# One kernel of feed-forward, token mixing and feed-forward: four pieces of work moved in the mixing stage

## The chip, the cores and the metric

The kernel runs on one core of a Trainium2 chip. Its time is the device time of one launch in microseconds (us); the time before is 3143.79 us, the median of three runs (3139.49 to 3144.29).

A core has five engines that run side by side, each with its own list of instructions in a fixed order: TensorE (PE in the profile, with its weight loads as PEld), VectorE (DVE), ScalarE (ACT), GpSimd (POOL) and SyncE (SP, which here only issues DMAs). They meet at semaphores: an instruction that waits holds up all that stand behind it on its engine.

## The reference

Three layers act on 8192 tokens of 256 channels (8 sequences of 1024):

```
x = x + 0.5 * ffn(layernorm(x))      # 16 experts, top 2 of them per token, capacity 1280 rows each
x = x + attn(layernorm(x))           # token mixing, RWKV-6
x = x + 0.5 * ffn(layernorm(x))      # the same experts once more
```

The middle layer is the one that the change touches:

```
xx  = previous token - x                       # "differences"
xxx = x + xx * maa_x
lora = tanh(xxx @ maa_w1)                      # 5 strips of 32
xf  = x + xx * (maa_f + lora_f @ maa_w2_f)     # f = w, k, v, r, g: the five mixes
r, k, v = xr @ Wr, xk @ Wk, xv @ Wv
g = tanh(xg @ gate_w1) @ gate_w2               # the gates
w = exp(-exp(time_decay + tanh(xw @ decay_w1) @ decay_w2))
y_t = r_t (S + u k_t v_t);  S = w_t S + k_t v_t     # one state of 64 x 64 per head, 4 heads
out = (groupnorm(y) * ln_g + ln_b) * g @ Wo
```

The router of the third layer (layernorm, logits over 16 experts, top 2, place in the expert) is computed in the same stage, on the rows that the mixing has finished.

## The kernel before

The program is a row of stages: constants, routing a, experts a, mixing together with routing b (`mix_and_route`), experts b. Only the mixing stage is changed. In the profiled execution it lies from about 1205 to 2215 us.

The stage works in 16 groups of 512 tokens (`NG`, `GT`), four tiles of 128 rows each. It is a software pipeline written out by hand: for step s in -2 to 18, each engine runs a fixed list of pieces for five groups at once. X = s+2 is the group that comes in (layernorm, transposition, differences, first mixes), F = s+1 gets its other mixes, keys, values, queries and decays, L = s goes through the eight levels of the products inside a tile, K = s-1 gets states, outputs, gates and Wo, R = s-2 is routed, and Z = s-3 has its rows scattered to the experts' slots. The order of the `if live(..)` blocks in each engine's loop is the order of execution; no scheduler stands behind it.

What ties the engines within a step:

- The levels. `level(L, n)` on TensorE (L1757) needs `take(n-1)` on VectorE (copy_predicated, L1203 for n=0, L1208 for the others) and the two multiplications `decay_right` and `decay_left` (L1221, L1232; together `factors`). `factors(L, n)` in its turn needs `level(L, n+1)`. So TensorE and VectorE hand the work to and fro eight times in a step, and the rest of both engines' work is put between.
- The PSUM banks. Four banks, a to d, serve all products; the list `order` says which product uses which bank after which. Each `fill` waits until the product before it in its bank is drained. Here it matters that "L" (the router's logits) follows "Y0" in bank b, where Y0 is drained by ScalarE's square (L1607), and that "V0" and "V1" (the values) follow "M8" and "M9" (the two halves of the last mix, for r), which are drained by VectorE's `mix_in` (L1179).
- The last mix. `mixes_of_rest` (L1857) writes M8 and M9 in two passes with a wait on `rest_half` between them.
- Buffers. `xx` exists once: `differences(X)` (L1167 and two of L1171) overwrites what `mix_in(F, 8)` and `mix_in(F, 9)` still read, and so stands behind them.
- GpSimd's list in the middle of a step: four indirect DMAs of the routed rows (L1515), the additions of mixes 8 and 9 (`mix_add`, L1464), the gate product `gate(K)` (L1504: Y times G), the root of the variances (L1487), four more indirect DMAs, and the additions of mixes 0 to 3.
- ScalarE's list: it copies the finished outputs Y (L1606) and their squares (L1607), then the logits, values and queries. In the first half of the step it copies keys (L1630), normalises the group that comes in (L1575) and copies transposed rows out of PSUM (L1563), the routed ones (`untie(ROUTE, ..)`, to `m_ygT`) after `keys` and `normalise`.

## Time and profile before

| | us |
|---|---|
| time, median of 3 | 3143.79 |
| the profiled execution's own time | 3144.1 |
| its span in the trace | 3142.4 |
| TensorE busy | 2773.4 (88%) |
| VectorE busy | 2017.5 (64%) |
| ScalarE busy | 1572.8 (50%) |
| GpSimd busy | 1256.9 (40%) |

The shares are those of the whole span. The two expert stages take some 1900 us of it, nearly all with TensorE busy. A change of the mixing stage has to be read from the steps of that stage. In the trace's lines the program's names stand with their stage's prefix, so `m_xx` is `xx` of the mixing stage; a line in brackets behind an instruction gives the idle time of its engine just before it and what ended it. The granted clock (PEclk) is TensorE's, as a share of its full speed.

### The profile page before, as it was taken

Reading aid. Unit: us, or ns where it says so; the run is one execution under the profiler, and the core shown is the slowest. Engines: PE = TensorE matmul, PEld = TensorE weight load, DVE = VectorE, ACT = ScalarE, POOL = GpSimd, SP = SyncE. Lnnn points to the kernel's source line nnn. Section 1 sums busy time; section 2 is a strip of 40 time slices with the busy share of each in tenths; the row PEclk is TensorE's granted clock in tenths of the full one; section 3 lists DMA queues with packets and bytes.
Section 4 is the critical chain, followed back from the end, with each engine's and each line's share of the span. In section 5 each row is a group of like instructions: output and inputs, shape, how many; then the busy total and the mean of one; then the engine's idle time right before and its main releaser. Section 6 shows DMA issues by size and latency. Waiting matters only on the chain. (4 is left out here: it accounts for less than half of the span.)

```text
span 3142.4 us, 63449 instructions
## 1 busy us (share of the span) xinstructions
PE 2773.4 (88%) x21936; PEld 2236.8 (71%) x21936; DVE 2017.5 (64%) x4620; ACT 1572.8 (50%) x2733; POOL 1256.9 (40%) x1072
## 2 busy tenths in 40 slices
PE   6354999999999995899899999974899999999997
PEld 6343888888888882566566666653788888888886
DVE  5354665666666653688888888863566666666664
ACT  5232665656665652344444444421556656656653
POOL 2652332222322223456676666644122322223233
PEclk9999999999999997999999999966899999999998
DMA  9924454544545527101111111001644545545444
GB/s 344 310 74 107 87 95 80 89 87 86 88 80 88 94 28 260 50 21 39 41 43 36 49 36 43 31 30 46 125 87 86 92 78 89 90 85 87 79 75 146
DMA packets 540964, 281.26 MB, mean 90 GB/s; under 512 B 397591, under 2 KB 503131, under 8 KB 540480
## 3 DMA queue, kind: packets, MB, share of 16 engines
q1 hardware_dynamic: 478624, 202.67, 25.8%
q0 software_dynamic: 57888, 75.16, 14.0%
q8 instruction: 127, 2.08, 0.3%
q10 hardware_dynamic: 4224, 0.52, 0.1%
q14 instruction: 101, 0.83, 0.1%
HBM read 150.83 MB, written 146.41 MB: 95 GB/s over the span
## 5 line engine op out<-in xcount | busy, mean ns | idle before, releaser
L763 POOL DMA_INDIRECT acc_a<-ae_ob,ae_to x160 | 260.2, 1626 | 675.7 <-ACT ae_ob L712 623.2
L763 POOL DMA_INDIRECT acc_b<-be_ob,be_to x150 | 243.5, 1623 | 636.3 <-ACT be_ob L712 534.0
L730 ACT ACTIVATE be_h<-be_pH,b 128x512 f32<-128x512 f32 (+1 forms) x384 | 236.8, 617 | 359.8 <-PE be_pH L657 334.4
L730 ACT ACTIVATE ae_h<-ae_pH,b 128x512 f32<-128x512 f32 (+1 forms) x384 | 236.8, 617 | 344.8 <-PE ae_pH L657 327.6
L1464 POOL TENSOR_TENSOR m_xf<-m_tmp,m_xT 128x512 f32<-128x512 f32 x160 | 181.3, 1160 | 150.6 <-DVE m_tmp L1179 150.5
L1757 PEld LDWEIGHTS m_PP<-m_RP,m_KS 64*64 64x64 f32 x6656 | 124.2, 142 | 106.9 <-issue 105.8
L1757 PE MATMUL m_PP<-m_RP,m_KS 64*64 64x64 f32 x6656 | 139.4, 229 | 56.3 <-DVE m_A L1208 49.4
L1515 POOL DMA_INDIRECT slots_b<-m_row,m_sidx x128 | 137.7, 1076 | 117.7 <-issue 117.7
L464 POOL DMA_INDIRECT slots_a<-ar_row,ar_sidx x128 | 125.8, 982 | 130.8 <-issue 105.9
L1179 DVE SCALAR_TENSOR_TENSOR m_tmp<-m_B,m_ch,m_xx 128x512 f32<-128x512 f32 x160 | 111.9, 741 | 71.3 <-PE m_B L1847 37.9
L657 PE MATMUL ae_pH<-ae_xT0h,ae_w_0h 128*128 128x512 f32 (+1 forms) x256 | 88.1, 344 | 53.8 <-DVE ae_xT0l L839 51.4
L684 PE MATMUL be_pO<-be_w,be_hT3h 128*128 128x512 f32 x320 | 118.5, 400 | 4.2 <-DVE be_hT3l L856 4.1
L1221 DVE TENSOR_TENSOR m_RP<-m_RP,m_tot 128x512 f32<-128x512 f32 x96 | 95.4, 994 | 39.3 <-PE m_PP L1757 31.4
L684 PE MATMUL be_pO<-be_w,be_hT0h 128*128 128x512 f32 x320 | 119.0, 402 | 1.3 <-DVE be_hT0l L856 1.2
L684 PE MATMUL ae_pO<-ae_w,ae_hT0h 128*128 128x512 f32 x320 | 118.5, 401 | 1.4 <-DVE ae_hT0l L856 1.3
L684 PE MATMUL be_pO<-be_w,be_hT1h 128*128 128x512 f32 x320 | 117.3, 397 | 1.8 <-DVE be_hT1l L856 1.7
L684 PE MATMUL ae_pO<-ae_w,ae_hT3h 128*128 128x512 f32 x320 | 117.1, 396 | 0.1
L684 PE MATMUL ae_pO<-ae_w,ae_hT1h 128*128 128x512 f32 x320 | 117.1, 396 | 0.0
L684 PE MATMUL be_pO<-be_w,be_hT2h 128*128 128x512 f32 x320 | 117.0, 396 | 0.0
L684 PE MATMUL ae_pO<-ae_w,ae_hT2h 128*128 128x512 f32 x320 | 117.0, 396 | 0.0
L657 PE MATMUL be_pH<-be_xT0h,be_w_0h 128*128 128x512 f32 (+1 forms) x256 | 88.2, 344 | 32.6 <-DVE be_xT0l L839 30.8
L856 DVE TENSOR_TENSOR ae_hT0l<-ae_h,ae_hT0h 128x512 fp32r<-128x512 f32 (+1 forms) x96 | 57.9, 603 | 90.0 <-ACT ae_hT0h L730 90.0
(343 smaller groups left out, 9009.5 us busy)
## 6 DMA issues: line engine op xcount, KB each, us to landing
ae_stage<-in_w SPq DMA_DIRECT2D x64, 512.0 KB, 3.5
be_stage<-in_w SPq DMA_DIRECT2D x64, 512.0 KB, 3.6
slots_a<-empty SPq DMA_DIRECT2D x5, 4160.0 KB, 25.0
slots_b<-empty SPq DMA_DIRECT2D x5, 4160.0 KB, 31.5
ae_xq<-slots_a SPq DMA_DIRECT2D x252, 64.0 KB
be_xq<-slots_b SPq DMA_DIRECT2D x252, 64.0 KB
ar_xin<-in_x SPq DMA_DIRECT2D x16, 512.0 KB, 10.1
m_xin<-acc_a SPq DMA_DIRECT2D x16, 512.0 KB, 4.8
```

Source lines behind the costliest of these rows:

```text
L464: pool.indirect_dma_start(S.slots[tag][:, :], bass.IndirectOffsetOnAxis(ap=sidx[u][:, q, k:k + 1], axis=0), row[u][:, q, :], None, bounds_ ...
L657: t = pe.matmul(pH[c % 2][:, 0:SIZES[b]], w1[u][a][:, k, f * P:(f + 1) * P], xT[(u * BLOCKS + b) % 2][z][:, k, 0:SIZES[b]], start=(n == 0) ...
L684: pe.matmul(to[:, q % 2, :], hT[s][HI][:, ts], w2[u][:, f, :, :].rearrange("p s d -> p (s d)"), start=(f == 0), stop=(f == FC - 1), skip_g ...
L730: t = act.activation(dst[:, 0:SIZES[b]], pH[c % 2][:, 0:SIZES[b]], ACT.Gelu, bias=S.b1[:, bass.ds(i * (2 * FC) + (u * FC + f), 1)])
L763: pool.indirect_dma_start(S.acc[tag][:, :], bass.IndirectOffsetOnAxis(ap=to[m][:, q:q + 1], axis=0), ob[m][:, q, :], None, bounds_check=T ...
L856: dve.tensor_tensor(hT[s][LO][:, 0:SIZES[b]], h32[c % 2][:, 0:SIZES[b]], hT[s][HI][:, 0:SIZES[b]], ALU.subtract).then_inc(h_split, 1)
L1179: drains(dve.scalar_tensor_tensor(out=tmp[m % TMP][:, :], in0=bank(f"M{m}", g)[:, :], scalar=ch[:, 1 + f, k:k + 1], in1=xx[:, k, :], op0=A ...
L1221: dve.tensor_tensor(rp[:, :, 1, :], rp[:, :, 1, :], pieces(l)[:, :, 0:1].to_broadcast([P, DC * GT >> (l + 1), 1 << l]), ALU.mult).then_inc ...
L1464: pool.tensor_tensor(xf[f][:, k, :], tmp[m % TMP][:, :], xT[g % 2][:, k, 1:GT + 1], ALU.add).then_inc(mixed, 1)
L1515: pool.indirect_dma_start(S.slots["b"][:, :], bass.IndirectOffsetOnAxis(ap=sidx[w][:, q, k:k + 1], axis=0), row[w][:, q, :], None, bounds_ ...
L1757: t = pe.matmul(PP[c * N:c * N + N, h, to], ks[rows, r, ts], rp[rows, r, ss], start=True, stop=True, skip_group_check=True)
```

## The change

Four pieces move; no instruction is added or taken away.

1. VectorE: `differences(X)` goes ahead of `mix_in(F, 8..9)`. For this `xx` is doubled, and `xxx` gets no buffer of its own any more but uses `wl`, the buffer of the clamped decays. Two waits come with it: `differences` waits for `w_ready` (the decays of the group before are read out of `wl`), `clamp` for "LG" (the products that read `xxx` are done). The wait for M9 of the group before goes.
2. GpSimd: `gate(K)` goes ahead of the additions of mixes 8 and 9. Two of the four DMAs in front of it go to the block behind the root.
3. TensorE: the logits stand between the two passes of `mixes_of_rest`.
4. TensorE and ScalarE: the routed rows are turned, and copied out, ahead of the keys; beside it the first decay product (`rate(F, 0)`) goes ahead of `level(L, 2)`.

```diff
-        xx = sb("xx", [P, DC, GT])
-        xxx = sb("xxx", [P, DC, GT])
+        xx = [sb(f"xx{u}", [P, DC, GT]) for u in range(2)]
...
+        xxx = wl[:, :].rearrange("p (c t) -> p c t", c=DC)
...
                 def differences(g):
                     untied(dve, IN, g)
-                    drained(dve, "M9", g - 1)
...
                     filled(dve, "LG", g - 1)
+                    hold(dve, w_ready, g)
...
                 def clamp(g, k):
                     hold(dve, w_ready, g)
+                    filled(dve, "LG", g)
...
                     keep(L, 4)
+                    if live(X):
+                        differences(X)
                     if live(F):
                         for m in range(8, 10):
                             mix_in(F, m)
-                    if live(X):
-                        differences(X)
...
                     if live(Z):
-                        scatter(Z, (0, 1))
+                        scatter(Z, (0,))
+                    if live(K):
+                        gate(K)
                     if live(F):
                         for m in range(8, 10):
                             mix_add(F, m)
                     if live(K):
-                        gate(K)
                         root_spread(K)
                     if live(Z):
-                        scatter(Z, (2, 3))
+                        scatter(Z, (1, 2, 3))
...
+                    if live(R):
+                        filled(act, "O1", K - 1)
+                        untie(ROUTE, R, xTr[:, :, :])
                     if live(F):
                         keys(F)
                     if live(X):
                         normalise(X)
-                    if live(R):
-                        filled(act, "O1", K - 1)
-                        untie(ROUTE, R, xTr[:, :, :])
...
-                    if live(L):
-                        level(L, 2)
                     if live(F):
                         rate(F, 0)
+                    if live(L):
+                        level(L, 2)
                     if live(L):
                         gates(L, 0)
+                    if live(R):
+                        turn_route(R)
                     if live(F):
                         project(F, "K", Wk, 1)
-                    if live(R):
-                        turn_route(R)
...
                     if live(F):
-                        mixes_of_rest(F)
+                        mixes_of_rest(F, 0)
                     if live(R):
                         logits(R)
+                    if live(F):
+                        mixes_of_rest(F, 1)
```

VectorE in the middle of a step, before, from the factors of level 3 to those of level 4:

```order
L1221 TENSOR_TENSOR m_RP<-m_RP,m_tot 128x64x8
L1232 TENSOR_TENSOR m_KS<-m_KS,m_tot 128x64x8
L1208 COPY_PREDICATED m_A<-m_lev,m_PP 128x64x8
L1179 SCALAR_TENSOR_TENSOR m_tmp<-m_B,m_ch,m_xx 128x512 x2
L1167 TENSOR_TENSOR m_xx<-m_xT 128x1024
L1171 SCALAR_TENSOR_TENSOR m_xxx<-m_xx,m_ch,m_xT 128x512 x2
L1255 TENSOR_REDUCE m_var<-m_Y 128x16
L1258 TENSOR_SCALAR m_mvar<-m_var 128x16
L1221 TENSOR_TENSOR m_RP<-m_RP,m_tot 128x32x16
```

The same stretch of VectorE in the changed kernel, where two lines of code more stand ahead of these (so L1223 is what L1221 was) and `m_wl` holds `xxx`:

```order
L1223 TENSOR_TENSOR m_RP<-m_RP,m_tot 128x64x8
L1234 TENSOR_TENSOR m_KS<-m_KS,m_tot 128x64x8
L1210 COPY_PREDICATED m_A<-m_lev,m_PP 128x64x8
L1167 TENSOR_TENSOR m_xx<-m_xT 128x1024
L1172 SCALAR_TENSOR_TENSOR m_wl<-m_xx,m_ch,m_xT 128x512 x2
L1180 SCALAR_TENSOR_TENSOR m_tmp<-m_B,m_ch,m_xx 128x512 x2
L1257 TENSOR_REDUCE m_var<-m_Y 128x16
L1260 TENSOR_SCALAR m_mvar<-m_var 128x16
L1223 TENSOR_TENSOR m_RP<-m_RP,m_tot 128x32x16
```

The subtraction and the two instructions for `xxx` have passed the two of the last mix. GpSimd in the same part of the step, before:

```order
L1497 TENSOR_TENSOR m_G<-m_G,m_ln_g 128x1024
L1515 DMA slots_b<-m_row,m_sidx 20480x260 x4
L1464 TENSOR_TENSOR m_xf<-m_tmp,m_xT 128x512 x2
L1504 TENSOR_TENSOR m_Y<-m_Y,m_G 128x1024
L1487 TENSOR_TENSOR m_rvar<-m_mvar,m_minus_half 128x16
L1515 DMA slots_b<-m_row,m_sidx 20480x260 x4
```

GpSimd in the changed kernel:

```order
L1499 TENSOR_TENSOR m_G<-m_G,m_ln_g 128x1024
L1517 DMA slots_b<-m_row,m_sidx 20480x260 x2
L1506 TENSOR_TENSOR m_Y<-m_Y,m_G 128x1024
L1466 TENSOR_TENSOR m_xf<-m_tmp,m_xT 128x512 x2
L1489 TENSOR_TENSOR m_rvar<-m_mvar,m_minus_half 128x16
L1517 DMA slots_b<-m_row,m_sidx 20480x260 x6
```

The gate product has passed the additions, and two DMAs have gone behind the root. TensorE between levels 4 and 5, before:

```order
L1757 MATMUL m_PP<-m_RP,m_KS 64x64 x32
L1819 MATMUL m_B<-m_St,m_RP 128x64 x16
L1857 MATMUL m_B<-m_lorag,m_maa_w2r 128x256 x4
L1926 MATMUL m_B<-m_ygT,m_rw 32x128 x8
L1897 MATMUL m_B<-m_Wv,m_xf 128x256 x8
```

TensorE in the changed kernel:

```order
L1760 MATMUL m_PP<-m_RP,m_KS 64x64 x32
L1822 MATMUL m_B<-m_St,m_RP 128x64 x16
L1861 MATMUL m_B<-m_lorag,m_maa_w2r 128x256 x2
L1929 MATMUL m_B<-m_ygT,m_rw 32x128 x8
L1861 MATMUL m_B<-m_lorag,m_maa_w2r 128x256 x2
L1900 MATMUL m_B<-m_Wv,m_xf 128x256 x8
```

The four products of the last mix are parted two and two, with the logits (`m_rw`) between them. In the trace each of these products shows as two records, so a count there is twice the one here.

## Rows read from the trace of the kernel before

**Rows 1.** Timeline of VectorE: start us, us, engine, line; first copy of steps 1 and 14
```profile
1307.53 1.31 DVE L1203 COPY_PREDICATED m_A<-m_diag,m_PP 128x1024 f32<-128x1024 int32 x1 [0.45 <-PE m_PP L1757]
...
2016.39 1.31 DVE L1203 COPY_PREDICATED m_A<-m_diag,m_PP 128x1024 f32<-128x1024 int32 x1 [0.47 <-PE m_PP L1757]
```
**Rows 2.** Timeline of TensorE in step 5 (1522 to 1577 us), middle part
```profile
1543.40 1.16 PE L1757 MATMUL m_PP<-m_RP,m_KS 64*64 64x64 f32 x64
...
1546.42 0.70 PE L1857 MATMUL m_B<-m_lorag,m_maa_w2r 32*128 32x256 f32 x4
1547.99 0.70 PE L1857 MATMUL m_B<-m_lorag,m_maa_w2r 32*128 32x256 f32 x4 [0.87 <-PE m_B L1857]
1548.62 0.64 PE L1926 MATMUL m_B<-m_ygT,m_rw 128*32 128x128 f32 x16
1549.62 3.69 PE L1897 MATMUL m_B<-m_Wv,m_xf 128*128 128x256 f32 x16 [0.35 <-DVE m_tmp L1179]
1553.24 1.16 PE L1757 MATMUL m_PP<-m_RP,m_KS 64*64 64x64 f32 x64
...
1560.53 1.79 PE L1757 MATMUL m_PP<-m_RP,m_KS 64*64 64x64 f32 x64 [2.43 <-DVE m_A L1208]
...
1567.94 1.09 PE L1765 MATMUL m_PT<-ident,m_Y 128*128 128x128 f32 x8
```
**Rows 3.** Timeline of VectorE in the same step
```profile
1544.68 0.69 DVE L1221 TENSOR_TENSOR m_RP<-m_RP,m_tot 128x512 f32<-128x512 f32 x1 [0.40 <-PE m_PP L1757]
...
1545.89 0.68 DVE L1208 COPY_PREDICATED m_A<-m_lev,m_PP 128x512 f32<-128x512 int32 x1
1548.72 1.41 DVE L1179 SCALAR_TENSOR_TENSOR m_tmp<-m_B,m_ch,m_xx 128x512 f32<-128x512 f32 x2 [2.14 <-PE m_B L1857]
1550.23 5.50 DVE L1167 TENSOR_TENSOR m_xx<-m_xT 128x1024 f32<-128x1024 f32 x1
1555.77 1.42 DVE L1171 SCALAR_TENSOR_TENSOR m_xxx<-m_xx,m_ch,m_xT 128x512 f32<-128x512 f32 x2
...
1558.46 0.69 DVE L1221 TENSOR_TENSOR m_RP<-m_RP,m_tot 128x512 f32<-128x512 f32 x1
```
**Rows 4.** Timeline of GpSimd in the same step
```profile
1546.64 0.97 POOL L1515 DMA_INDIRECT slots_b<-m_row,m_sidx  x1 [0.30 <-issue]
...
1550.17 2.17 POOL L1464 TENSOR_TENSOR m_xf<-m_tmp,m_xT 128x512 f32<-128x512 f32 x2
1552.27 2.38 POOL L1504 TENSOR_TENSOR m_Y<-m_Y,m_G 128x1024 f32<-128x1024 f32 x1
```
**Rows 5.** The subtraction over all steps: ns min/median/max, first and last start us
```profile
L1167 DVE TENSOR_TENSOR m_xx<-m_xT x16: 1225/4956/5503, 1217.4 to 1990.4; 128x1024 f32<-128x1024 f32 x16
```
**Rows 6.** Timeline of ScalarE in the same step: outputs Y and their squares
```profile
1547.77 0.60 ACT L1607 ACTIVATE m_Y<-m_B 128x512 f32<-128x512 f32 x1
1548.26 0.59 ACT L1606 COPY m_Y<-m_B 128x512 f32<-128x512 f32 x1
```
**Rows 7.** Timeline of TensorE in the next step, first half
```profile
1584.09 1.16 PE L1757 MATMUL m_PP<-m_RP,m_KS 64*64 64x64 f32 x64 [0.82 <-DVE m_A L1208]
...
1593.58 1.07 PE L1765 MATMUL m_PT<-ident,m_KR 128*128 128x128 f32 x8 [0.60 <-ACT m_ygT L1563]
```
**Rows 8.** Timeline of TensorE in a late step
```profile
1880.61 5.92 PE L1897 MATMUL m_B<-m_Wv,m_xf 128*128 128x256 f32 x16
...
1891.24 0.97 PE L1757 MATMUL m_PP<-m_RP,m_KS 64*64 64x64 f32 x50
```
**Rows 9.** Stretches: busy us (count) by engine, then PEclk, DMA share, GB/s
```profile
1562.00:1565.00 3.00, 3.00 (x16) 1.41 (x11) 2.76 (x10) 0.19 (x1) 2.25 (x3) 0.63 0.14 50
1878.00:1885.00 7.00, 6.56 (x30) 4.63 (x31) 5.20 (x3) 2.57 (x6) 6.37 (x6) 0.52 0.16 57
```
**Rows 10.** Timelines of VectorE and GpSimd in an early step without row scatters
```profile
1388.97 4.23 DVE L1171 SCALAR_TENSOR_TENSOR m_xxx<-m_xx,m_ch,m_xT 128x512 f32<-128x512 f32 x2
...
1389.85 2.80 POOL L1504 TENSOR_TENSOR m_Y<-m_Y,m_G 128x1024 f32<-128x1024 f32 x1
```

More of the change, by code:

```diff
@@ L1849, in mixes_of, with mixes_of_rest @@
                                            tile_position=(32 * j, 0)), f"M{m}", g)
[L1851 removed]
+                def mixes_of_rest(g, a):
                     drained(pe, "LG", g)
[L1853 to L1863 removed]
+                    if a:
+                        pe.wait_ge(rest_half, g * 2 + 2)
+                    for k in range(DC):
+                        j = k ^ a
+                        b = bank(f"M{8 + k}", g) if a else fill(f"M{8 + k}", g)
+                        t = pe.matmul(b[:, j * GT // 2:(j + 1) * GT // 2], maa_w2r[32 * j:32 * j + 32, k * P:(k + 1) * P],
+                                      lorag[32 * j:32 * j + 32, :], start=True, stop=True, tile_position=(32 * j, 0))
+                        if a:
+                            fills_up(t, f"M{8 + k}", g)
+                        else:
+                            t.then_inc(rest_half, 1)
                 def narrow(g):
```

18 lines of the change are left out of this document (4 added, 14 removed).

## The prediction

> **What bounds the kernel now.** I first took the page's engine shares: TensorE is the fullest engine, but in the mixing stage the work goes to and fro between TensorE and VectorE, so shares say little, and I went on to the timelines of a step. The first copy of a step starts at 1307.53 in step 1 and at 2016.39 in step 14 [rows 1]: 13 steps in 708.9 us, 54.5 us each. All of this is on the path, since the experts of the last layer start when the stage has ended. Only steps 1 to 13 have both a group that comes in and a gate product, so only there do the first two moves bear together.
>
> In step 5 the reader is to follow one chain. Level 4 starts on TensorE at 1543.40, the two passes of the last mix at 1546.42 and 1547.99 with 0.87 idle between them, the logits at 1548.62, the values at 1549.62 after a wait for VectorE, level 5 at 1553.24. Level 6 then waits 2.43 us for VectorE [rows 2]. VectorE was late because its subtraction took 5.50 us [rows 3], while the same instruction takes 1.225 us at its shortest [rows 5]. It started at 1550.23, when GpSimd had just begun two additions and the gate product behind them (1550.17 to 1554.65) [rows 4]; it ended at 1555.73, about 1.1 us after the last of these. So the subtraction stood still while GpSimd worked, and then ran at its usual speed.
>
> Behind the 2.43 us wait level 6 takes 1.79 us, other levels 1.16 [rows 2], and from 1562 to 1565 the granted clock averages 0.63: TensorE, which had stood idle, had fallen from 2.4 to 1.2 GHz for part of the time [rows 9]. In late steps it goes otherwise: the clock falls in the sparse stretch of the last mix and the logits (0.52 on average from 1878 to 1885 [rows 9]), the values take 5.92 instead of 3.69 us, and level 6 follows without a wait [rows 8]. The step is as long either way.
>
> **The change part by part.** No instruction is added, so what counts are waits.
>
> *Differences ahead, gate ahead.* VectorE's copy of level 3 ends at 1546.57 and it then idles 2.14 us [rows 3]; the subtraction and `xxx` fit there: 1.22 + 1.42 = 2.64 us, if nothing blocks them. GpSimd does only DMAs then [rows 4]. The new waits for `w_ready` and "LG" are for work finished earlier. The last mix may then start on VectorE at 1549.2 at the soonest. Behind it only `spread` is left before level 5's factors, which leaves the 5.50 + 1.42 us of [rows 3] out of that place. Six DMAs instead of four stand behind the root; GpSimd has idle time behind them, cost 0.
>
> *Logits between the passes.* This looks like a filler for the 0.87 us. But the logits use the bank of Y0 and must wait for ScalarE's square, which ends at 1547.77 + 0.60 = 1548.37 [rows 6]; the second pass started at 1547.99 before [rows 2] and now comes only behind the logits. So this edit delays it: logits at 1548.37, 0.63 long (1547.99 to 1548.62 is the pass, 1548.62 to 1549.25 the logits by the same measure), second pass at 1549.0, 1.0 us later than before. Between the start of the second pass and `mix_in` lie 1548.72 - 1547.99 = 0.73 us, and from there to the values 0.90 us: the values at 1550.63, 1.0 us later than 1549.62. The bounds: the 0.87 us gained if Y0 is drained before the first pass ends, 1.0 lost as computed; I take the loss of 1.0, since its rows stand in this step.
>
> *Rows ahead of the keys, decay product ahead of level 2.* In the next step level 2 waits 0.82 us for VectorE, and the transposition of the incoming rows 0.60 us for ScalarE's copy of the routed ones [rows 7]. The decay product fills idle time, the copy leaves the place between normalisation and transposition. The keys come 1.0 us later and so does ScalarE's normalisation in part. Bounds 0 and 0.6; no such wait stands in step 5, so I take 0.3.
>
> *The sum for a step.* Level 4 and all behind it move by -0.3, the values by +1.0 beside: they start at 1550.3, and level 5 at 1553.24 + 0.7 = 1553.94. Factors 4 follow a level's start by 1544.68 - 1543.40 = 1.28: 1555.22 instead of 1558.46 [rows 2, 3]. From these factors to the transposition of Y VectorE works without a gap worth naming, 1567.94 - 1558.46 = 9.48: now 1564.70. That is 3.2 us earlier. TensorE has level 6 at 1553.94 + (7.29 - 2.43) = 1558.80 and keeps up if its clock is high.
>
> *The clock.* The sparse stretch from level 4's end to the values gets longer and has two waits: for the square, and 0.9 for the first `mix_in`. The rows of late steps show a fall just there. Its cost is 0 at least; at most 2.23 (values, 5.92 against 3.69) and some 1.0 for the second pass and logits at half rate, 3.2 in all. The nearest rows are the values' own, so I take 2.2. Net: 3.2 - 2.2 = 1.0 us a step, 13 steps, 13 us. The profiled execution took 3144.1 us (span 3142.4 and 1.7 around it), 0.3 above the median, which I leave out: 3131.
>
> **The rivals.**
>
> *The clock stays up.* For it: step 5 had a high clock through this same stretch with idle time of 1.2 us. Against: the stretch is now emptier. Then 3.2 x 13 = 42 us: 3102.
>
> *The step keeps its length.* The clock takes back all of it. For it: waits before level 6 and slow values are exchanged for each other in the trace and the step stays at 54.5. Cost 3.2 of 3.2: 3144.
>
> *`xxx` is blocked by the gate product.* This ends slower. In an early step the two instructions of `xxx` took 4.23 us while the gate product started at 1389.85 beside them, 2.80 long [rows 10]: one of them waited for it. In the changed kernel the gate product no longer stands behind additions and starts when the second copy of Y is done, 1548.85 - 0.3 = 1548.55 [rows 6]. The second `xxx` instruction starts at 1546.2 (a copy's 0.6 behind, 0.3 earlier) + 1.26 + 0.71 = 1548.2. It wins by some 0.35 us. If the gate product's request comes before the first `xxx` instruction ends at 1548.2, the second waits for 2.38 us, ends at 1551.3, the values start 0.9 later at 1552.2 instead of 1550.3: 1.9 us later. With the clock's full 3.2 that is 3.2 - 1.9 - 3.2 = -1.9 a step, or 25 us: 3169; with 2.2 for the clock it is -0.9, or 12 us: 3156. I put it at 3160, between them. It decides if Y is ready 0.35 us sooner or the differences start that much later. The Trainium skill, page "SBUF — State Buffer", section "SBUF: two separate sides", says that a VectorE instruction with two SBUF inputs and a GpSimd instruction that reads SBUF contend for one pair of ports as an exclusive lock, held for the whole instruction by whichever started first. By that rule the move only changes who meets whom, and every step in which the gate product comes first pays; the trace agrees with the blocking (5.50 against 1.225).
>
> **How the numbers follow.** Apart from 0.2% (6.3 us; less than that is no change for this measurement) the boundary lies at 3137.5 and 3150.1. The forecast has 0.43, of it 0.37 faster and 0.06 within the bound; the high clock 0.17, all faster; the unchanged step 0.20, 0.18 of it the same and 0.02 slower; the blocked `xxx` 0.20, 0.19 slower and 0.01 the same. Sum: faster 0.54, same 0.25, slower 0.21. The likeliest case alone reaches from 3118 to 3140. The range leaves out half of the high clock's case and half of the blocked one: 3104 to 3158.
>
> **What the profile after would show.** Right: the subtraction at 1.2 to 1.5 us right behind level 3's copy; no wait of 2.4 us before level 6; the logits after 1 to 1.5 us of idle TensorE behind the first pass, their releaser ScalarE's square; the values at 5 to 6 us in most steps; first copies 53 to 54 us apart. Wrong: `xxx` at over 3 us for its two instructions (blocked), values at 3.7 in all steps and copies 51.3 apart (high clock), copies still 54.5 apart, or a new wait that none of this names, such as level 4's take behind the keys or level 5 behind a blocked `spread`.

## The result, and the profile after

The changed kernel takes 3254.59 us (median of four runs, 3250.09 to 3257.55), the kernel before 3143.00 beside it: a ratio of 1.0356, 95% interval 1.0338 to 1.0374. It is slower by 112 us, where 13 us faster was predicted and 3158 was the end of the range. The profiled execution has a span of 3251.0 us, 108.6 more than before. By the first copies of the steps, 5.4 us of this are lost ahead of step 0 (two traces of the kernel before differ there by 6.8) and 103.4 between step 0 and step 15 (907.9 us instead of 804.5). The last stage is as long as it was.

First copies of the steps (VectorE's timeline: start, duration, then what ended the idle time before). They answer to [rows 1]:

```profile
1319.19 1.32 DVE L1205 COPY_PREDICATED m_A<-m_diag,m_PP 128x1024 f32<-128x1024 int32 x1 [0.45 <-PE m_PP L1760]
...
1554.44 1.31 DVE L1205 COPY_PREDICATED m_A<-m_diag,m_PP 128x1024 f32<-128x1024 int32 x1 [0.47 <-PE m_PP L1760]
1616.95 1.31 DVE L1205 COPY_PREDICATED m_A<-m_diag,m_PP 128x1024 f32<-128x1024 int32 x1 [0.47 <-PE m_PP L1760]
...
2117.50 1.32 DVE L1205 COPY_PREDICATED m_A<-m_diag,m_PP 128x1024 f32<-128x1024 int32 x1 [0.47 <-PE m_PP L1760]
```

Steps 1 to 13 take 61.4 us each instead of 54.5, step 5 takes 62.5. The first of them do not: 55.6 in step 1 and 54.7 in step 2 (52.3 and 52.6 before), and 62.5 from step 3 on. Step 3 is the first with a group Z whose rows are scattered. So two losses can be told apart at sight: 2 to 3 us a step that is there without DMAs, and a jump of 7.8 us from step 2 to step 3, when the DMAs come, where the kernel before jumps by 2.1.

Step 5 on TensorE, as in [rows 2]:

```profile
1576.27 1.16 PE L1760 MATMUL m_PP<-m_RP,m_KS 64*64 64x64 f32 x64
...
1579.29 0.70 PE L1861 MATMUL m_B<-m_lorag,m_maa_w2r 32*128 32x256 f32 x4
1580.70 0.64 PE L1929 MATMUL m_B<-m_ygT,m_rw 128*32 128x128 f32 x16 [0.71 <-ACT m_Y L1610]
1581.27 0.70 PE L1861 MATMUL m_B<-m_lorag,m_maa_w2r 32*128 32x256 f32 x4
1585.17 5.86 PE L1900 MATMUL m_B<-m_Wv,m_xf 128*128 128x256 f32 x16 [3.20 <-DVE m_tmp L1180]
1590.95 1.08 PE L1760 MATMUL m_PP<-m_RP,m_KS 64*64 64x64 f32 x49
1592.41 0.35 PE L1760 MATMUL m_PP<-m_RP,m_KS 64*64 64x64 f32 x6 [0.38 <-issue]
...
1594.32 3.60 PE L1883 MATMUL m_B<-m_xf,m_Wr 128*128 128x512 f32 x8
1601.06 1.16 PE L1760 MATMUL m_PP<-m_RP,m_KS 64*64 64x64 f32 x64 [3.15 <-DVE m_A L1210]
```

The same step on VectorE [rows 3], and then on GpSimd [rows 4]:

```profile
1579.36 1.22 DVE L1167 TENSOR_TENSOR m_xx<-m_xT 128x1024 f32<-128x1024 f32 x1
1580.61 3.75 DVE L1172 SCALAR_TENSOR_TENSOR m_wl<-m_xx,m_ch,m_xT 128x512 f32<-128x512 f32 x2
1584.28 1.40 DVE L1180 SCALAR_TENSOR_TENSOR m_tmp<-m_B,m_ch,m_xx 128x512 f32<-128x512 f32 x2
...
1586.84 0.43 DVE L1260 TENSOR_SCALAR m_mvar<-m_var 128x16 f32<-128x16 f32 x1
1599.01 0.69 DVE L1223 TENSOR_TENSOR m_RP<-m_RP,m_tot 128x512 f32<-128x512 f32 x1 [11.74 <-remote]
```

```profile
1581.44 2.36 POOL L1506 TENSOR_TENSOR m_Y<-m_Y,m_G 128x1024 f32<-128x1024 f32 x1
1585.10 2.14 POOL L1466 TENSOR_TENSOR m_xf<-m_tmp,m_xT 128x512 f32<-128x512 f32 x2 [1.30 <-DVE m_tmp L1180]
1587.35 2.93 POOL L1489 TENSOR_TENSOR m_rvar<-m_mvar,m_minus_half 128x16 f32<-128x16 f32 x1
1590.48 1.06 POOL L1517 DMA_INDIRECT slots_b<-m_row,m_sidx  x1 [0.20 <-issue]
...
1596.95 0.97 POOL L1517 DMA_INDIRECT slots_b<-m_row,m_sidx  x1 [0.30 <-issue]
```

The subtraction takes 1.22 us where the prediction put it. Then three things go wrong. `xxx` takes 3.75 us for its two instructions, with the gate product beside it: 2.33 more than the 1.42 of [rows 3], as long as the gate product. The values wait 3.20 us for the mix behind it and then run at a low clock (5.86 us). And the factors of level 5 start 8.06 us behind the start of level 5, where 1.28 us was usual. VectorE waits 11.74 us; the label `remote` names no instruction that would have ended the wait. By the matmul rows level 5 has been over since 1594.2. VectorE starts 1.1 us after the last of six DMAs has ended on GpSimd (1596.95 + 0.97 = 1597.92). Inside that chain level 5 itself had stopped, after 49 of its 64 matmuls, three times for 0.4 us (one of the pauses is shown, as `issue`).

ScalarE is late in the same way. It waits for the queries, of which the first four matmuls are over at 1596.2:

```profile
1599.18 0.58 ACT L1640 COPY m_RP<-m_B 128x512 f32<-128x512 f32 x1 [7.53 <-remote]
```

The trace also has the time at which each semaphore was raised. Level 5's increment stands at 1598.98, those of the three products behind it at 1599.02 to 1599.14, and nothing else that these factors wait for changed while VectorE stood. So the work was done, and the news of it came late, all of it at once.

The page's group of these factors, and the granted clock around the values (window, length, TensorE's busy time, clock, DMA share, GB/s), to be held against [rows 9]:

```profile
L1223 DVE TENSOR_TENSOR m_RP<-m_RP,m_tot 128x512 f32<-128x512 f32 x96 | 92.4, 962 | 197.1 <-remote 145.0
```

```profile
1581.00:1585.00 4.00, 0.97 (x19) 0.72 0.10 35
1585.00:1591.00 6.00, 5.83 (x20) 0.62 0.01 3
```

145 us of VectorE's idle time ahead of the factors are of the `remote` kind; before it was 6.8.

### The profile page after: what moved, and what is told of

Same layout as the page of the kernel before. It is cut to its first block and busy times, and to the rows that moved or that the text cites. A ratio compares the mean times of both kernels' runs of the same rounds, so it can differ in the third digit from the quotient of the medians.

```text
span 3251.0 us, 63451 instructions
## 1 busy us (share of the span) xinstructions
PE 2822.6 (87%) x21936; PEld 2261.2 (70%) x21936; DVE 1987.2 (61%) x4620; ACT 1572.3 (48%) x2733; POOL 1247.2 (38%) x1072
## 5 line engine op out<-in xcount | busy, mean ns | idle before, releaser
L1760 PEld LDWEIGHTS m_PP<-m_RP,m_KS 64*64 64x64 f32 x6656 | 131.6, 144 | 133.7 <-issue 131.9
L1760 PE MATMUL m_PP<-m_RP,m_KS 64*64 64x64 f32 x6656 | 152.1, 232 | 70.1 <-DVE m_A L1210 50.2
L1223 DVE TENSOR_TENSOR m_RP<-m_RP,m_tot 128x512 f32<-128x512 f32 x96 | 92.4, 962 | 197.1 <-remote 145.0
L1900 PE MATMUL m_B<-m_Wv,m_xf 128*128 128x256 f32 x256 | 92.7, 540 | 49.3 <-DVE m_tmp L1180 49.3
L657 PE MATMUL ae_pH<-ae_xT0h,ae_w_0h 128*128 128x512 f32 (+1 forms) x256 | 87.8, 343 | 54.0 <-DVE ae_xT0l L839 51.5
L1900 PEld LDWEIGHTS m_B<-m_Wv,m_xf 128*128 128x128 f32 x256 | 71.2, 285 | 72.1 <-issue 56.5
```

Of the source, the lines that this page charges most:

```text
L657: t = pe.matmul(pH[c % 2][:, 0:SIZES[b]], w1[u][a][:, k, f * P:(f + 1) * P], xT[(u * BLOCKS + b) % 2][z][:, k, 0:SIZES[b]], start=(n == 0) ...
L1223: dve.tensor_tensor(rp[:, :, 1, :], rp[:, :, 1, :], pieces(l)[:, :, 0:1].to_broadcast([P, DC * GT >> (l + 1), 1 << l]), ALU.mult).then_inc ...
L1760: t = pe.matmul(PP[c * N:c * N + N, h, to], ks[rows, r, ts], rp[rows, r, ss], start=True, stop=True, skip_group_check=True)
L1900: t = pe.matmul(b[:, q * D:(q + 1) * D], xf[2][:, k, ts], Wv[:, k, :], start=(k == 0), stop=(k == 1))
```

## The experiments

**What was to be told apart.** Theory 1, the hold: while GpSimd issues a chain of indirect DMAs, TensorE is held back, in its matmuls or in the increments by which VectorE learns that they are done; the change laid a chain of six beside level 5. Theory 2: the new order on VectorE makes the loss, by way of the blocked `xxx` and the clock. The measure that separates them best is the time from the first copy of step 0 to that of step 15, 15 steps, which neither end of the program enters.

**The chips differ, and that has to be said first.** The variants ran on four chips (that of the two first traces is not on record). On three of them the kernel before takes 3143 to 3146 us, on the one of a_nodma, b_nodma, a_split22 and a_diffback 3081.55; it is called the fast chip here. A ratio is always to the runs of before on the same chip. The column "15 steps" is the time in us from the first copy of step 0 to that of step 15 in the trace, the last one the shortest and longest of the steps 3 to 13.

| run | what it is | us | ratio (95%) | 15 steps | steps 3 to 13 |
|---|---|---|---|---|---|
| before, first trace | | 3143.0 | | 804.5 | 54.6-56.3 |
| b_again | before, second trace | 3140.3 | | 805.2 | 54.2-56.2 |
| after, first trace | | 3254.6 | 1.0356 (1.0338-1.0374) | 907.9 | 62.3-63.3 |
| a_again | after | 3247.3 | 1.0316 (1.0298-1.0333) | 900.7 | 59.8-62.8 |
| a_third | after | 3247.4 | 1.0328 (1.0306-1.0350) | 897.7 | 59.6-62.8 |
| a_nodma, fast chip | after, no DMAs | 3111.8 | 1.0098 (1.0081-1.0115) | 815.2 | 54.4-56.3 |
| a_nodma_2 | after, no DMAs | 3145.2 | 1.0002 (0.9990-1.0014) | 814.9 | 54.5-56.1 |
| b_nodma, fast chip | before, no DMAs | 3069.4 | 0.9964 (0.9953-0.9975) | 778.2 | 52.6-54.3 |
| a_nodma_diff | no DMAs, VectorE as before | 3103.7 | 0.9867 (0.9839-0.9896) | 781.0 | 52.1-53.8 |
| a_nodma_gate | no DMAs, gate as before | 3098.2 | 0.9846 (0.9829-0.9864) | 770.2 | 51.0-51.5 |
| a_split22, fast chip | after, DMAs 4 + 4 | 3099.4 | 1.0061 (1.0044-1.0078) | 791.1 | 51.9-54.1 |
| a_split22_2 | after, DMAs 4 + 4 | 3198.3 | 1.0172 (1.0150-1.0194) | 855.4 | 56.5-58.1 |
| a_diffback, fast chip | after, VectorE as before | 3082.1 | 1.0007 (0.9994-1.0020) | 785.1 | 52.2-54.1 |
| a_diffback_2 | after, VectorE as before | 3217.6 | 1.0227 (1.0200-1.0253) | 870.1 | 55.4-62.1 |
| b_split13 | before, DMAs 2 + 6 | 3193.8 | 1.0156 (1.0134-1.0179) | 840.2 | 54.8-64.0 |
| b_split31 | before, DMAs 6 + 2 | 3149.4 | 1.0013 (0.9998-1.0027) | 808.4 | 53.7-56.7 |
| a_split31 | after, DMAs 6 + 2 | 3189.5 | 1.0132 (1.0099-1.0166) | 838.4 | 55.9-56.6 |
| a_spaced | after, DMAs with gaps | 3230.7 | 1.0268 (1.0250-1.0285) | 879.2 | 57.5-63.0 |
| a_thin | after, DMAs of 8 numbers a row | 3249.0 | 1.0329 (1.0296-1.0362) | 903.5 | 61.6-62.8 |
| a_diffback_31 | VectorE as before, DMAs 6 + 2 | 3174.7 | 1.0101 (1.0085-1.0118) | 826.1 | 55.5-57.4 |

### Without the DMAs

a_nodma and b_nodma: `scatter` does nothing, and the waits on `scattered` are out. a_nodma_2 is a_nodma on another chip.

```diff
                 def scatter(g, qs):
-                    w = g % RING
...
+                    pass
...
-                        dve.wait_ge(scattered[w], g // RING * (16 * GQ * TOPK))
...
-                        act.wait_ge(scattered[w], g // RING * (16 * GQ * TOPK))
```

> The changed kernel, but the routed rows are never scattered in the mixing stage (the work left out are the eight indirect DMAs of a step and the waits on them). Theory 1 (the hold): while GpSimd issues its six DMAs in a row, TensorE's semaphore increments reach VectorE only behind the last of them, and this makes the 11.7 us of VectorE's idle time ahead of the factors of level 5. Without DMAs steps 3 to 13 fall from 62.5 to the length that steps 1 and 2 of the changed kernel have (54.7 to 55.6), the idle time ahead of these factors falls under 3 us, and the time is some 85 to 95 us shorter, 3160 to 3170. Theory 2 (the order of VectorE and the blocked xxx cost the time, and the low clock at the values): steps stay above 60, the time above 3230. That the last expert stage finds empty slots may change its own time, so the steps decide, not the total.

> The kernel before without the scattering of the routed rows in the mixing stage (the same work left out). It gives the measure for the changed kernel without it. Theory 1: there is some hold in the kernel before too (0.5 to 1 us behind the first four DMAs, none that matters behind the others), and steps 3 to 13 fall from 54.7 to what steps 1 and 2 have, 52.4, so about 3115 to 3120. The difference of the two kernels without scattering is then 2 to 3 us a step, the part of the loss that has nothing to do with the DMAs. Theory 2: the difference stays 7 to 8 us a step.

> The changed kernel without the scattering in the mixing stage (that work left out), once more. Its steps can't depend on the hold: 54.4 to 54.9 in steps 3 to 13 on either chip. On a chip of 3145 us the total is then 3155 to 3165, the ratio 1.003 to 1.007: that is the loss of the change without any hold, less the DMAs' own time.

Theory 1 had the steps right: 54.4 to 54.9 in most and 52.6 in most, and the changed kernel's on both kinds of chip (815.2 and 814.9 us for its 15 steps). The totals expected of the first two were for a chip of 3144 us and can't be held against the fast one; that of a_nodma_2 came out below what was expected, since the last stage is some 20 us shorter with empty slots. In 15 steps the DMAs cost the changed kernel 907.9 - 814.9 = 93.0 us, and the kernel before 804.5 - 778.2 = 26.3. So of the 103.4 us that the change costs, 66.7 go with the DMAs and 814.9 - 778.2 = 36.7 have nothing to do with them. With a_third, which ran on the chip of a_nodma_2, the 66.7 are 56.5 (897.7 in place of 907.9). b_nodma ran on the fast chip alone; that its steps would be the same on another is taken from a_nodma and a_nodma_2.

### The part without DMAs: the blocked xxx

a_nodma_diff, on top of a_nodma, puts VectorE's list back; a_nodma_gate leaves VectorE changed and puts the gate product back behind the additions.

```diff
-                    if live(X):
-                        differences(X)
                     if live(F):
                         for m in range(8, 10):
                             mix_in(F, m)
+                    if live(X):
+                        differences(X)
```

> The changed kernel without scattering (that work left out) and with VectorE's list as before. The changed kernel without scattering has steps of 54.7, the kernel before without it 52.6; this tells which move makes the 2.1 us that have nothing to do with DMAs. Theory 2a (the differences, of which xxx is blocked by the gate product and delays the last mix): steps of 52.0 to 52.6, ratio to the kernel before 0.985 to 0.989. Theory 2b (the logits between the passes and the early gate product themselves): steps stay at 54 to 55, 1.000.

```diff
-                    if live(K):
-                        gate(K)
                     if live(F):
                         for m in range(8, 10):
                             mix_add(F, m)
+                    if live(K):
+                        gate(K)
```

> The changed kernel without scattering (that work left out), and with the gate product behind the additions of the last mix, as before. VectorE keeps its new order, differences first. Shown so far: without DMAs the new order of VectorE makes steps of 54.7 where the old one has 52.4. Theory 2a (xxx is blocked by the gate product, so the last mix and the values start late): xxx takes 1.4 us again, mix_in starts 2 us earlier, the values wait under 1 us for it; steps of 52 to 53 or shorter, a ratio of 0.985 to 0.99. Theory 2c (the emptier stretch drops TensorE's clock whoever blocks whom, and the values then take 5 to 5.9 us): steps of 53.5 to 54.7, a ratio of 0.995 to 1.000.

Theory 2a had both times right, or nearly (0.9867 and 0.9846). With VectorE's list as before 33.9 of the 36.7 us are gone (781.0), so all other moves together cost 2.8 us. But the new order is not at fault by itself. With the gate product late it gives 770.2 us, 8.0 under the kernel before without DMAs and 44.7 under a_nodma_2: steps of 51.0 to 51.5. That the prediction's rival of the high clock had 51.3 is a coincidence: it took 3.2 us off steps of 54.5 with DMAs, here some 1.3 come off steps of 52.6 without. First a_nodma_2, a step's `xxx` on VectorE, the gate product and the values:

```profile
1561.54 3.50 DVE L1172 SCALAR_TENSOR_TENSOR m_wl<-m_xx,m_ch,m_xT 128x512 f32<-128x512 f32 x2
...
1562.04 2.46 POOL L1506 TENSOR_TENSOR m_Y<-m_Y,m_G 128x1024 f32<-128x1024 f32 x1 [8.94 <-ACT m_Y L1597]
...
1565.85 5.08 PE L1888 MATMUL m_B<-m_Wv,m_xf 128*128 128x256 f32 x16 [2.16 <-DVE m_tmp L1180]
```

then the same places of a_nodma_gate:

```profile
1607.00 1.41 DVE L1172 SCALAR_TENSOR_TENSOR m_wl<-m_xx,m_ch,m_xT 128x512 f32<-128x512 f32 x2
...
1609.29 3.69 PE L1888 MATMUL m_B<-m_Wv,m_xf 128*128 128x256 f32 x16 [0.93 <-DVE m_tmp L1180]
...
1611.32 2.36 POOL L1506 TENSOR_TENSOR m_Y<-m_Y,m_G 128x1024 f32<-128x1024 f32 x1
```

The gate product, started 0.5 us after the first instruction of `xxx`, holds the second for 2.1 us. From the first pass of the last mix to the values are 5.63 us in the one kernel (1560.22 to 1565.85) and 3.61 in the other (1605.68 to 1609.29), and the values themselves take 1.39 longer at the lower clock: 3.4 of the 3.7 us by which these two steps differ. The granted clock is 0.50 from 1562 to 1566 in the first kernel, 1.00 from 1605 to 1609 in the second, where the values take 3.69 us in all of the steps 3 to 13. For these steps theory 2c, that the emptier stretch drops the clock whoever blocks whom, fell. But in a_nodma_gate's steps -1 to 2 and 14 the values take 5.28 to 6.27 us, though `xxx` is free there too. And what drops the clock in a_nodma_2 is not the wait just ahead of the values alone: the logits before that wait are slow already (0.92 us against 0.65). What does it stays open.

What the block costs beside the DMAs can be read within one execution. In a_third `xxx` is free (1.41 us) in the steps 4, 6, 8, 10 and 12, and these take 59.6 to 60.8 us; in the other six from 3 to 13 it takes 3.75, and they take 62.6 to 62.8. So some 2.4 us of a step go with the block, and the hold is there without it.

### Does the loss depend on the chip

a_split22 (four and four) and a_diffback (VectorE as before) came first, on the fast chip; a_again, b_again and a_third are the two kernels themselves, a_split22_2 and a_diffback_2 the same variants once more.

```diff
                     if live(Z):
-                        scatter(Z, (0,))
+                        scatter(Z, (0, 1))
...
-                        scatter(Z, (1, 2, 3))
+                        scatter(Z, (2, 3))
```

> The changed kernel with the DMAs divided as before, four ahead of the gate product and four behind the root. Theory 1: the chain behind the root starts where it did and ends two DMAs, some 2.2 us, sooner, so TensorE's increments arrive 2 us sooner: steps of about 60.3, 3228 to 3236. The gate product starts some 2 us later, but the additions behind it wait for VectorE anyway. Theory 2: no change beyond 5 us, 3250 to 3260.

> The changed kernel with VectorE's list as before: the last two mixes ahead of the differences; all else as changed. Theory 1: the spread of the variances, and with it the root and the chain of six DMAs, come some 5 us later in the step, behind level 5 and its increment, so the long wait ahead of the factors of level 5 goes. The chain then holds level 7 or the transposition of Y, for 2 us more than the chain of four did: steps of 56 to 58, 3160 to 3185. Theory 2 (six DMAs cost GpSimd time wherever they stand, and the order of VectorE only 2 to 3 us a step): 3215 to 3230.

> The changed kernel itself, unchanged, beside the others of this series: the times of the four kernels above were taken beside runs of the kernel before at 3081.55 us, 62 us below its first ones, so the changed kernel has to be measured there too. Theory 1 (chains of six DMAs hold TensorE's increments): the same 7.8 us a step in steps 3 to 13, 1.03 to 1.04 times the kernel before. If the long wait is a matter of the one execution shown first, the ratio is 1.01 and the wait is not there.

> The kernel before, for its steps in the same conditions. All theories: the order of its work and its waits as in the first trace; steps of 53 to 54.7 us, some 12 us in all above the kernel without DMAs (52.6 each).

> The changed kernel once more, as the measure of the three beside it. The first four variants were run on a chip where the kernel before takes 3081.55 us, the later ones on one where it takes 3145.84. In the four traces from the former VectorE never waits long for an increment of TensorE that comes late; in all traces with six DMAs in a row from the latter it does. Two readings. Theory A (the chip decides): one chip holds TensorE's increments back behind GpSimd's DMAs, the other doesn't. Theory B (the kernel decides): the variants that ran there happened to have no chain of six. If this run falls on a chip of 3145 us: a ratio of 1.03 to 1.036 by both. If it falls on one of 3082 us: 1.005 to 1.012 by theory A, 1.03 to 1.04 by theory B.

> The changed kernel with its DMAs four and four, once more. On a chip of 3145 us: by theory A the chain of four behind the root, which still stands beside level 5, holds its increment too: VectorE waits 5 to 9 us, steps of 58 to 60, a ratio of 1.015 to 1.025. By theory B chains of four hold nothing, steps of 52 to 54: 1.00 to 1.01. On a chip of 3082 us: 1.006 again.

> The changed kernel with VectorE's list as before, once more. On a chip of 3145 us: by theory A the chain of six stands behind level 6, as in the kernel before with DMAs divided two and six, so steps of 55 to 62 and a ratio of 1.01 to 1.02; by theory B too. If it comes out at 1.00, the hold needs level 5 in the chain. On a chip of 3082 us: 1.00 again.

On the fast chip a_split22 had steps of 52 to 54 where 60.3 was expected, and a_diffback 3082.1 us in all where either theory had over 3160. I read into the first that four DMAs in a row do nothing. That was wrong. The same kernel on another chip has 58.1. This is its level 6, beside the chain of four behind the root (first and last of it), on that chip:

```profile
1694.97 0.91 PE L1760 MATMUL m_PP<-m_RP,m_KS 64*64 64x64 f32 x42
1696.26 0.35 PE L1760 MATMUL m_PP<-m_RP,m_KS 64*64 64x64 f32 x4 [0.38 <-issue]
1697.02 0.31 PE L1760 MATMUL m_PP<-m_RP,m_KS 64*64 64x64 f32 x2 [0.42 <-issue]
1697.74 0.21 PE L1760 MATMUL m_PP<-m_RP,m_KS 64*64 64x64 f32 x1 [0.41 <-issue]
1698.45 0.63 PE L1760 MATMUL m_PP<-m_RP,m_KS 64*64 64x64 f32 x15 [0.49 <-issue]
...
1692.78 1.07 POOL L1517 DMA_INDIRECT slots_b<-m_row,m_sidx  x1 [0.20 <-issue]
...
1696.70 0.97 POOL L1517 DMA_INDIRECT slots_b<-m_row,m_sidx  x1 [0.30 <-issue]
```

and this the same place on the fast chip, with a chain that starts at 1542.38:

```profile
1544.63 1.16 PE L1760 MATMUL m_PP<-m_RP,m_KS 64*64 64x64 f32 x64
...
1542.38 1.06 POOL L1517 DMA_INDIRECT slots_b<-m_row,m_sidx  x1 [0.20 <-issue]
```

64 matmuls take 4.1 us instead of 1.16, with four pauses of 0.4 us, in the one case and none in the other: the same instructions, the same DMAs beside them. Counted over the stage, the traces with all their DMAs on the other chips have 9 to 43 such pauses inside the levels in the variants and the changed kernel, 1 and 3 in the kernel before, and each lies inside a DMA of GpSimd or within 0.7 us of one. The two of the fast chip (a_split22, a_diffback) have none, like the five traces without DMAs. Nor have they an increment of TensorE that comes over 0.6 us after its matmul's end; each of the others has 19 or more, the kernel before too. Theory A holds for these variants: the chip decides. Theory B is out: a_diffback has a chain of six on the fast chip too, and only there is it free (1.0007 against 1.0227). The changed kernel itself never ran on the fast chip, so what it takes there is not known. Of the two kernels once more, a_again came as expected (1.0316, VectorE's long waits are there), b_again's steps a little above it. The expectation of a_third for a chip of 3145 us came true, and that for a_split22_2 too in the ratio, but not in place: VectorE waits only 1.85 us for level 5, and it is level 6 that stands. a_diffback_2 came out above its range (1.0227 against 1.01 to 1.02): moving VectorE's work back by 5 us only changes which level the six DMAs meet.

### How many DMAs, where, and with what in them

b_split13 makes the kernel before issue two and six, b_split31 six and two, a_split31 the changed kernel six and two.

```diff
-                        scatter(Z, (0, 1))
+                        scatter(Z, (0,))
...
-                        scatter(Z, (2, 3))
+                        scatter(Z, (1, 2, 3))
```

> The kernel before with its eight DMAs divided as in the changed one, two ahead of the additions and six behind the root; nothing else. Dividing four and four removed the whole hold in the changed kernel (steps of 52 to 54 instead of 62.5), far more than the 2 us that two DMAs take, so it is not the time of the DMAs that counts but how many stand in one chain. Theory 1: six in a row hold back TensorE here too. The chain starts at about the transposition of the outputs, 3 to 6 us behind level 6, and holds what TensorE finishes in it, the second half of the outputs and level 7: 2 to 6 us a step, 3105 to 3150. Theory 3 (the hold needs the chain and level 5 at one time, since level 5 follows with 64 small matmuls on a TensorE that has no other finished work to hand on): 3075 to 3090, no change.

> The changed kernel with six DMAs ahead of the gate product and two behind the root. In the split of four and four TensorE's level 6 stood still four times for 0.4 us inside the chain behind the root; in the changed kernel it is level 5. Theory 1 (a chain costs only where TensorE has a level of 64 small matmuls, or something that VectorE waits for, in it): the chain of six now lies beside the last mix, the logits and the values, the levels are nearly free of it: steps of 53 to 56, a ratio of 0.99 to 1.01. Rival (a chain of six costs 5 to 8 us wherever it stands, since every increment of TensorE is held): the values' mixes are late, steps of 59 to 62, a ratio of 1.02 to 1.03.

> The kernel before with six DMAs ahead of the additions and two behind the root; nothing else. The additions and the gate product come 2.7 us later, behind the subtraction, which is no longer blocked (1.2 us instead of 5.5), so level 6 need not wait its 2.4 us. Theory 1: steps of 52.5 to 54, 3110 to 3135, faster than the kernel before by 0.3 to 1%. Rival (the chain of six holds the passes of the last mix and the logits): steps of 57 to 60, a ratio of 1.01 to 1.02.

b_split13 moves two DMAs in the kernel before, nothing else, and loses 1.56%, some 48 us, within the 23 to 68 us that theory 1 gave it above 3081.55 (35.7 us in the 15 steps of the trace, which is that of the fastest of its runs). Level 6, TensorE and then the factors behind it on VectorE:

```profile
1509.19 0.92 PE L1757 MATMUL m_PP<-m_RP,m_KS 64*64 64x64 f32 x47
1510.31 0.33 PE L1757 MATMUL m_PP<-m_RP,m_KS 64*64 64x64 f32 x3 [0.19 <-issue]
...
1518.59 0.69 DVE L1221 TENSOR_TENSOR m_RP<-m_RP,m_tot 128x512 f32<-128x512 f32 x1 [7.42 <-remote]
```

The chain runs from 1509.75 to 1517.18, and VectorE goes on 1.4 us after it. This is the changed kernel's wait, made in the kernel before by its scatter blocks alone, here beside level 6, and theory 3 (it needs level 5) fell. It is not the same in every step (54.8 to 64.0).

a_split31 and b_split31 put six DMAs where no level is. Neither expectation fits a_split31 (1.0132): the levels 4 and 5 are whole there, but the last two DMAs stop level 6 again:

```profile
1528.05 0.92 PE L1760 MATMUL m_PP<-m_RP,m_KS 64*64 64x64 f32 x45
1529.18 0.35 PE L1760 MATMUL m_PP<-m_RP,m_KS 64*64 64x64 f32 x4 [0.22 <-issue]
...
1527.92 1.06 POOL L1517 DMA_INDIRECT slots_b<-m_row,m_sidx  x1 [0.20 <-issue]
1529.29 0.97 POOL L1517 DMA_INDIRECT slots_b<-m_row,m_sidx  x1 [0.30 <-issue]
```

So two are enough. b_split31 fits neither of its expectations either. The subtraction is free (1.29 us on average instead of 3.8), and nothing is gained by it: 1.0013. In four of the steps 3 to 13 `xxx` is blocked in its place (5.84 us), but where both are free the steps take 53.7 to 56.7 us, as in the kernel before.

One caution on a_split22_2: it changes more than the length of the chain. The gate product comes two DMAs later, so `xxx` is free in 14 of 16 groups, and the chain starts 1.6 to 2.7 us behind level 5's start in all but one of the steps 3 to 13 and meets level 6. The 42.3 us between it and a_third (897.7 - 855.4) are not the price of two DMAs more in a row alone.

a_spaced writes 256 elements a partition behind each of the six DMAs, each waiting for the write before; a_thin keeps the chains and shrinks what they carry.

```diff
                                 oob_is_err=False).then_inc(scattered[w], 16)
+                            if q:
+                                pool.wait_ge(spared, S.spaces)
+                                pool.memset(spare[:, :], 0.0).then_inc(spared, 1)
+                                S.spaces += 1
```

> The changed kernel with the same two and six DMAs, and behind each of the six a small write of GpSimd (256 elements a partition, into a buffer that nobody reads), which the next DMA stands behind. Theory 1a (what holds TensorE's increments is a row of DMA instructions without a break): the breaks let the increments through, VectorE's wait ahead of the factors of level 5 falls from 11.7 to under 4 us and steps to 54 to 56: a ratio of 1.005 to 1.015. Theory 1b (what counts is how many DMAs are under way, more than four, whatever stands between): the hold stays and gets 1 to 3 us longer, a ratio of 1.03 to 1.05.

```diff
-                                S.slots["b"][:, :], bass.IndirectOffsetOnAxis(ap=sidx[w][:, q, k:k + 1], axis=0),
-                                row[w][:, q, :], None, bounds_check=E * CAP - 1,
+                                S.thin[:, :], bass.IndirectOffsetOnAxis(ap=sidx[w][:, q, k:k + 1], axis=0),
+                                row[w][:, q, 0:8], None, bounds_check=E * CAP - 1,
```

> The changed kernel with the same eight indirect DMAs in the same places, but each writes 8 numbers of a row in place of 260, into a tensor of its own (so what is left out is that the routed rows reach the last experts). Theory 1c (TensorE is held by the bytes that the six DMAs move): the hold goes, steps of 54.7 as without DMAs, a ratio of 1.000 to 1.005. Theory 1d (it is held by GpSimd's making of so many descriptors, whatever they carry): steps of 60 to 63 as before, a ratio of 1.025 to 1.035.

a_thin is clear: 1.0329, the same as the changed kernel (1.0328 and 1.0316), with a thirtieth of the bytes. VectorE's wait ahead of the factors of level 5, and the last DMA of the chain before it:

```profile
1595.41 0.69 DVE L1223 TENSOR_TENSOR m_RP<-m_RP,m_tot 128x512 f32<-128x512 f32 x1 [11.95 <-remote]
...
1593.13 0.97 POOL L1517 DMA_INDIRECT thin_b<-m_row,m_sidx  x1 [0.31 <-issue]
```

The bytes that the DMAs move do not hold TensorE. What is left is their issuing on GpSimd, or their number, which a_thin keeps; no run tells these apart. a_spaced fell between its two theories (1.0268). The longest waits are as before, but many end inside the chain, while the fourth of the six DMAs runs:

```profile
1699.36 1.06 POOL L1518 DMA_INDIRECT slots_b<-m_row,m_sidx  x1 [0.20 <-issue]
...
1703.85 0.97 POOL L1518 DMA_INDIRECT slots_b<-m_row,m_sidx  x1 [0.17 <-issue]
...
1704.58 0.69 DVE L1224 TENSOR_TENSOR m_RP<-m_RP,m_tot 128x512 f32<-128x512 f32 x1 [8.43 <-remote]
```

The gap from one DMA to the next is 0.5 us here (1700.42 to 1700.92) and 0.3 in the plain chain. It lets something through, but not at once. Whether a gap, or a certain number of finished DMAs, ends the hold is open.

### The attempt at a better kernel

a_diffback_31 joins the edits of a_diffback and a_split31.

> All moves of the changed kernel but the one of the differences, and with six DMAs ahead of the gate product and two behind the root. It joins what was best in each pair. Theory 1 (making descriptors costs only beside the levels and beside what VectorE or ScalarE waits for): no level has a DMA beside it but level 6 or 7 with two; steps of 53 to 54, a ratio of 0.990 to 0.997. Rival (every chain costs some 2 us a step by small delays and by TensorE's clock, as in the kernel before with the same split): steps of 54.5 to 55, a ratio of 0.999 to 1.003.

It is slower than both expectations, 1.0101. The second pass of the last mix lies in the chain of six now, and its increment is late: `mix_in` starts 1.80 us after it (1611.74 to 1613.54), where 0.73 was usual. The values then wait for it, and pay by the clock:

```profile
1611.74 0.70 PE L1861 MATMUL m_B<-m_lorag,m_maa_w2r 32*128 32x256 f32 x4
1614.43 6.58 PE L1900 MATMUL m_B<-m_Wv,m_xf 128*128 128x256 f32 x16 [1.99 <-DVE m_tmp L1180]
...
1613.54 1.41 DVE L1180 SCALAR_TENSOR_TENSOR m_tmp<-m_B,m_ch,m_xx 128x512 f32<-128x512 f32 x2 [3.61 <-PE m_B L1861]
```

`xxx` is blocked in nine of the 16 groups besides (5.83 us and a little more). None of the variants with all their DMAs beats the kernel before. What a_nodma_gate suggests, differences first, the gate product behind the additions and the DMAs where they hold nothing, was not run with DMAs.

## Why the prediction was wrong

*Six DMAs instead of four stand behind the root, "cost 0".* This is the step that failed. It asked only whether GpSimd has time for them. Three things moved at once. The root came earlier, since the differences ahead of `spread` are no longer late (in step 5 11.1 us behind level 4's start instead of 15.2). Level 5 came later, behind the blocked `xxx` and slow values (14.7 us behind level 4's instead of 9.8). And the chain behind the root got longer. In the kernel before it starts 6.1 to 9.0 us behind level 5's start and lies beside level 7 or 6, in the changed kernel between 1.2 us ahead and 0.3 behind, beside level 5 in each of the steps 3 to 13. In step 5 the factors come 8.06 us behind level 5's start instead of 1.28: 6.8 us, of the 7.8 by which the step is longer than step 2. In the 15 steps 66.7 of the 103.4 us go with the DMAs (56.5 by a_third). No rival named it.

*The blocked `xxx`.* The forecast had it win by 0.35 us; the third rival had it lose, at 1.9 us a step. It lost in 13 of 16 groups: `xxx` takes 52.4 us in the whole stage against 26.8 where it is blocked in two (a_split22_2, a_split31), 1.6 us a group. In a_third it lost in eight. In step 5 the gate product starts when the second DMA ahead of it has ended (1579.51 + 1.91 = 1581.42), within 0.1 us of the second `xxx` instruction's turn (1580.61 + 0.71 = 1581.32): too near for any forecast. The forecast had the gate product start when the second copy of Y is done; it counted no time for the DMAs ahead of it. With its consequences this makes 33.9 us in 15 steps; the rival had 12 to 25 us over 13. The mechanism was right, its chance of 0.20 too small.

*Differences unblocked, level 6's wait gone.* Right for the subtraction: 1.22 us in every step. The wait of 2.43 us [rows 2] came back as 3.15, as VectorE was late from the hold. The 3.2 us a step that the sum put on this are shown by no run: without DMAs and with `xxx` free it is some 1.3 (a_nodma_gate against b_nodma), and in b_split31, with DMAs, nothing.

*Logits between the passes delay the second by 1.0 us.* Mis-sized. The square was waited for (0.71), but the second pass starts 1.98 us after the first, against 1.57 before [rows 2]: 0.4 us. All moves but the differences together cost 2.8 us in 15 steps without DMAs.

*Rows ahead of the keys, 0.3 us gained.* Wrong in sign, small: from a first copy to level 4 are 21.83 us in step 5, and 21.57 in step 5 of the kernel before.

*The clock takes 2.2 us.* In step 5 right in size (the values 5.86 us instead of 3.69, 2.17), but not for the reason given. I put it down to the emptier stretch. a_nodma_gate has the same stretch, with a wait of 0.93 ahead of the values, and keeps the full clock in the steps 3 to 13. That the size was right is luck; the cause stays open.

The rule of the Trainium skill on the shared ports (page "SBUF — State Buffer", section "SBUF: two separate sides") was named for this blocking. The traces agree with it: in the changed kernel `xxx` is longer by 2.33 us beside a gate product of 2.36. Which of the two came first there, 0.1 us apart, the trace does not resolve.

## What to carry to other kernels

An indirect DMA on GpSimd is not free because GpSimd has time for it: where it is issued is a place in TensorE's schedule too, and a chain that comes to lie beside many small matmuls, or beside a result that another engine waits for, can cost more than all moves of the change bring (here 66.7 us in 15 steps). After an edit that makes anything ahead of such a chain earlier, look up what TensorE does during it. A variant that leaves the DMAs out shows in one run what the rest of a change is worth. Compare variants only on one chip.

## What the runs showed of the hardware that was not expected

- On three of the chips TensorE stops while GpSimd issues indirect DMAs: 64 small matmuls take 3 to 4 us instead of 1.16, in pauses of 0.4 us (3.1 us beside two DMAs of 1 us each in a_split31, 4.1 beside four in a_split22_2), and its increments come up to 5 us late (level 5's last matmul at 1594.2, its increment at 1598.98, in the changed kernel). It does not depend on the bytes (8 or 260 numbers a row: 903.5 and 897.7 to 907.9 us). Whether the matmuls stop for want of instructions or because their increments find no way is open; no run tells these apart.
- One chip of four showed none of it, in the two variants with DMAs that ran there. There the kernel before took 3081.55 us, 62 less, and the mixing stage's step 0 began at 1237 to 1242 us instead of 1260 to 1276. The stage ahead of it scatters rows in the same manner, and GpSimd idles less there ahead of its DMAs: 99 to 101 us in the four traces of the fast chip, 125 to 136 in all others. That this is the same hold is not shown. The first row is of the fast chip (a_nodma), the second of another (a_third); the columns are busy time, mean ns, and the idle time before with what ended it:

```profile
L464 POOL DMA_INDIRECT slots_a<-ar_row,ar_sidx x128 | 125.9, 984 | 99.4 <-issue 72.9 <-DMA slots_a<-empty 25.3 <-DVE ar_row L360 0.6
```

```profile
L464 POOL DMA_INDIRECT slots_a<-ar_row,ar_sidx x128 | 125.7, 982 | 130.0 <-issue 105.3 <-DMA slots_a<-empty 24.7
```

What differs between the chips was not found, and the fast one was met on one occasion only.
